# Feed-forward of a transformer layer: centred ternary weight, layer norm from the mean square, residual in one VectorE operation

## The chip, the cores and the metric

The kernel runs on one core of one Trainium2 chip. A core has a matrix engine (TensorE, "PE", with its weight loads listed as "PEld"), a vector engine (VectorE, "DVE"), an activation engine (ScalarE, "ACT"), a general engine (GpSimd, "POOL") and a queue that issues DMA transfers (SyncE, "SP"). Each engine works through its own list of instructions in order, and waits on semaphores where it needs another engine's result. The metric is the device time of one execution in microseconds.

## The reference, cut to what matters

The layer is an attention part followed by a feed-forward part. Only the feed-forward part, its layer norm and its residual are touched by the change:

```python
LN_EPS = 0.001; EPS = 1e-05; QB = 128.0
mu = jnp.mean(x, axis=-1, keepdims=True)
var = jnp.var(x, axis=-1, keepdims=True)
xn = (x - mu) * jax.lax.rsqrt(var + LN_EPS) * ln_gamma + ln_beta
beta = jnp.mean(jnp.abs(weight))
w_q = jnp.clip(ste_round(weight / (beta + EPS)), -1.0, 1.0)   # every weight is -1, 0 or 1
gamma = jnp.max(jnp.abs(xn))
xq = jnp.clip(xn * QB / gamma, -QB + EPS, QB - EPS)
y = jnp.einsum('bsd,du->bsu', xq, w_q)
return y * (gamma * beta / QB)

# around it, with x of shape (4, 4096, 512), float32
x = x + _layernorm(_L0_attn_ref(_layernorm(x), Wv, Wo, Wg, Wb))
x = x + _layernorm(_L0_ffn_ref(_layernorm(x), weight, ln_gamma, ln_beta))
```

`_layernorm` subtracts the mean over the last axis and divides by the root of the variance plus 1e-5.

## The kernel before, in words

The program has three stages, one after the other. `setup` loads the weights, splits the attention weights into two 16-bit parts, and makes the ternary weight `wq` (128 partitions x 4 x 512, 16 bit). `attention` makes the first residual sum and leaves it in DRAM (`x1_scratch`), with a scale and a shift for each row (`z_scale`) that stand for the layer norm ahead of the feed-forward part. `feed_forward` does the rest.

The 16,384 rows are 128 tiles of 128 rows x 512 columns. `feed_forward` takes them in 32 groups of G = 4 tiles. A group goes through these steps:

- load 1 MB of `x1` (SP, L1092), five steps ahead;
- `f_z` = x1 times scale plus shift, a tile at a time (DVE, L1230), three steps ahead;
- transpose `f_z` into the four banks `ps_z` (PE, L1273), two steps ahead, and from there scale by gamma and beta into `f_u` (ACT, L1151);
- one step ahead, the clip `f_uc` of the whole group (DVE, L1248, 128x2048), its 16-bit upper part (ACT, L1170) and the 16-bit remainder (DVE, L1259), both in `f_xq`;
- for each tile eight matmuls of 512 columns (4 blocks of the inner dimension, 2 parts) into one of the four banks `ps_f` (PE, L1285);
- the layer norm of `ps_f`: `bn_stats` and `bn_aggr` give mean and variance (DVE, L1209 and L1220); POOL makes the variance plus eps, the negated mean, the power -0.5 and the shift for two tiles at once (L1120, L1121, L1124, L1127); ACT applies scale and shift into `f_yn` (L1161); POOL adds the residual into `f_res` (L1133); SP stores `f_res` in four pieces (L1099).

The order of the work on each engine is written by hand in the functions `step`, and the semaphores named `f_...` count finished instructions. `step(base, j)` handles group j, and parts of groups j-1, j+1, j+2 and j+3. A matmul bank `ps_f[i]` is free again for the next group when ACT has written `f_yn` of tile i; PE starts a group when its remainder `f_lo` is there. The first 13 and the last 9 steps are written out and the 16 between run in a loop of 8.

Of the kernel before, what the change touches and what calls it, by code (L numbers as in the profile page):

```python
# [49 lines left out]
def setup(nc, io, k):  # L50

    with ExitStack() as ctx:
        def sb(name, shape, dt=F32):
# [20 lines left out]
        wo_mean = sb("wo_mean", [P, KB])  # L74
        above = sb("above", [P, KB, D])
# [9 lines left out]
        wo_summed, wo_meaned, wo_centred = sem("wo_summed"), sem("wo_meaned"), sem("wo_centred")  # L85

# [85 lines left out]
        def _(dve):  # L172
# [39 lines left out]

            dve.wait_ge(scaled, len(turns) + 1)
# [18 lines left out]
            dve.wait_ge(wq_s, 1)  # L232
# [789 lines left out]
def feed_forward(nc, io, k):  # L1022

    with ExitStack() as ctx:
# [3 lines left out]
        def sem(name):  # L1028
# [14 lines left out]
        sc = sb("f_sc", [P, 2, G, 2])  # L1043
# [4 lines left out]
        raw = sb("f_raw", [P, G, 6])  # L1048
        mv = sb("f_mv", [P, 2, G, 2])
        veps = sb("f_veps", [P, 2, 2])  # L1050
        neg = sb("f_neg", [P, 2, 2])
        ysc = sb("f_ysc", [P, 2, G, 2])
        yn = sb("f_yn", [P, G, D])
# [6 lines left out]
        names = """f_ends_g f_ends f_rowtop f_top f_inv f_scaled f_gb f_unit f_sc f_z f_zt f_u f_clip f_hi f_lo f_y  # L1060
            f_sums f_stats f_veps f_rstd f_ysc f_yn f_res""".split()
        s = {n: sem(n) for n in names}

        def run(eng, step):


            for j in range(-FLAG_LOAD, FBODY):
                step(None, j)
            with eng.Fori(1, NG // FBODY - 1) as base:
                for i in range(FBODY):  # L1070
                    step(base, i)
            for j in range(NG - FBODY, NG + 1):
                step(None, j)

        def on(base, step, lag):

            g = step + lag if base is None else base * FBODY + (step + lag)
            return g, (step + lag) % FBODY, not isinstance(g, int) or 0 <= g < NG
# [7 lines left out]
        @block.sync  # L1086
        def _(sp):
            def step(base, j):
                g, r, live = on(base, j, FLAG_LOAD)
                if live:  # L1090
                    wait(sp, s["f_res"], (g - (FBODY - 1)) * G)
                    sp.dma_start(x1[:, r, :, :], k["x1_dram"][bass.ds(g * G, G), :, :].rearrange("g p d -> p g d"))\  # L1092
                      .then_inc(loaded[r], 16)
                g, r, live = on(base, j, -1)
                if live:
                    sp.wait_ge(s["f_res"], g * G + G)
                    for b in range(B):
                        dst = io["out"][b, bass.ds(g * G * C, G * C), :].rearrange("(g t) d -> t g d", g=G)
                        sp.dma_start(dst, res[C * b:C * b + C, r % 2, :, :]).then_inc(stored[r % 2], 16)  # L1099
            run(sp, step)  # L1100
            for r in range(2):
                sp.wait_ge(stored[r], 16 * B * NG // 2)

        @block.gpsimd
        def _(pool):
# [4 lines left out]
            def half(base, j, lag, q):  # L1110

                g, r, live = on(base, j, lag)
                if not live:
                    return
                pair = slice(2 * q, 2 * q + 2)
                eps = y_eps[:, 0:1].to_broadcast([P, 2])

                pool.wait_ge(s["f_stats"], g * G + (2 * q + 2))
                wait(pool, s["f_yn"], (g - 1) * G)
                pool.tensor_tensor(veps[:, q, :], mv[:, r % 2, pair, 1], eps, ALU.add).then_inc(s["f_veps"], 1)  # L1120
                pool.tensor_tensor(neg[:, q, :], mv[:, r % 2, pair, 0], k["minus_one"][:, 0:1].to_broadcast([P, 2]),  # L1121
                                   ALU.mult).then_inc(s["f_veps"], 1)
                pool.wait_ge(s["f_veps"], g * 4 + (2 * q + 2))
                pool.tensor_tensor(ysc[:, r % 2, pair, 0], veps[:, q, :], k["neg_half"][:, 0:1].to_broadcast([P, 2]),  # L1124
                                   ALU.pow).then_inc(s["f_rstd"], 1)
                pool.wait_ge(s["f_rstd"], g * 2 + (q + 1))
                pool.tensor_tensor(ysc[:, r % 2, pair, 1], neg[:, q, :], ysc[:, r % 2, pair, 0], ALU.mult).then_inc(s["f_ysc"], 1)  # L1127

                for i in ((0,), (1, 2, 3))[q]:
                    pool.wait_ge(s["f_yn"], g * G + (i + 1))  # L1130
                    if i == 0 and (not isinstance(g, int) or g >= 2):
                        pool.wait_ge(stored[r % 2], (g - r % 2) * (8 * B))
                    pool.tensor_tensor(res[:, r % 2, i, :], yn[:, i, :], x1[:, r, i, :], ALU.add).then_inc(s["f_res"], 1)  # L1133

            def step(base, j):
                half(base, j, -1, 1)
                half(base, j, 0, 0)
            run(pool, step)

        @block.scalar  # L1140
        def _(act):
            act.wait_ge(s["f_gb"], 1)

            def inputs(base, j, blocks):

                g, r, live = on(base, j, FLAG_T)
# [7 lines left out]
            def outputs(base, j, lag, q):  # L1154

                g, r, live = on(base, j, lag)
                for i in (2 * q, 2 * q + 1) if live else ():
                    if i == 2 * q:
                        act.wait_ge(s["f_ysc"], g * 2 + (q + 1))
                    wait(act, s["f_res"], (g - 1) * G + (i + 1))  # L1160
                    nc.scalar.activation(yn[:, i, :], ps_f[i][:, :], ACT.Identity, scale=ysc[:, r % 2, i, 0:1],  # L1161
                                         bias=ysc[:, r % 2, i, 1:2]).then_inc(s["f_yn"], 1)

            def step(base, j):
                outputs(base, j, -1, 1)
                g, r, live = on(base, j, FLAG_CLIP)
# [4 lines left out]
                inputs(base, j, (0, 1))  # L1171
                outputs(base, j, 0, 0)
                inputs(base, j, (2, 3))
            run(act, step)

        @block.vector
        def _(dve):
# [24 lines left out]
            def sums(base, j, lag, i):  # L1202

                g, r, live = on(base, j, lag)
                if live:
                    dve.wait_ge(s["f_y"], g * G + (i + 1))
                    wait(dve, s["f_ysc"], g * 2 - 2)
                    wait(dve, s["f_stats"], (g - 1) * G + (i + 1))
                    dve.bn_stats(raw[:, i, :], ps_f[i][:, :]).then_inc(s["f_sums"], 1)  # L1209

            def summed(base, j, lag, i):

                g, r, live = on(base, j, lag)
                if live:
                    dve.wait_ge(s["f_sums"], g * G + (i + 1))

            def stats(base, j, lag, i):
                g, r, live = on(base, j, lag)
                if live:
                    dve.bn_aggr(mv[:, r % 2, i, :], raw[:, i, :]).then_inc(s["f_stats"], 1)  # L1220

            def norm(base, j, tiles):

                g, r, live = on(base, j, FLAG_Z)
# [8 lines left out]
            def step(base, j):
                sums(base, j, -1, 3)
                summed(base, j, -1, 3)
                g, r, live = on(base, j, FLAG_Z)
                if live:
                    wait(dve, s["f_z"], (g - 1) * G)
                    dve.tensor_copy(sc[:, r % 2, :, :].rearrange("p g c -> p (g c)"),
                                    k["z_scale"][:, bass.ds(g * (2 * G), 2 * G)]).then_inc(s["f_sc"], 1)  # L1240
                stats(base, j, -1, 2)
                stats(base, j, -1, 3)
                g, r, live = on(base, j, FLAG_CLIP)
# [5 lines left out]
                sums(base, j, 0, 0)  # L1249
                norm(base, j, (0, 1, 2))  # L1250
                sums(base, j, 0, 1)
                summed(base, j, 0, 1)
                norm(base, j, (3,))
                stats(base, j, 0, 0)
                stats(base, j, 0, 1)
# [4 lines left out]
                sums(base, j, 0, 2)  # L1260
            run(dve, step)

        @block.tensor
        def _(pe):
            def turn(base, j, kb):

                g, r, live = on(base, j, FLAG_T)
# [8 lines left out]
            def step(base, j):  # L1276
                g, r, live = on(base, j, 0)
                for i in range(G):
                    if live:
                        if i == 0:  # L1280
                            pe.wait_ge(s["f_lo"], g + 1)
                        wait(pe, s["f_yn"], (g - 1) * G + (i + 1))
# [5 lines left out]
                    turn(base, j, i)  # L1288
            run(pe, step)
# [43 lines left out]
```

## Time and profile before

| | |
|---|---|
| Time, median of 3 runs | 2510.26 us (2506.84 to 2511.02) |
| The profiled execution: its own time / its span | 2514.57 us / 2512.8 us |
| Busy share PE, DVE, ACT, POOL | 86%, 82%, 69%, 77% |
| Instructions | 146,586 |
| Mean granted TensorE clock | 0.945 of full |
| Feed-forward stage | from about 2055 us to the end of the span |

Times inside the span count from the span's start. "Busy" is the time in which an engine has an instruction in work; "idle before" is its time without one, put down to the last semaphore that released it. The page divides the span into 40 slices of 62.8 us; the feed-forward stage begins in the 33rd. Through most of attention PE's slices read nine tenths busy or more at the full clock. In the feed-forward stage they read seven or eight tenths, and the granted clock reads eight tenths.

### The profile page before, as it was taken

How to read it: one execution, taken by the hardware profiler on the slowest of the kernel's cores; microseconds unless marked ns; L12 is line 12 of the kernel's file. 1: busy time of each engine (PE TensorE's matmuls, PEld its weight loads, DVE VectorE, ACT ScalarE, POOL GpSimd, SP SyncE). 2: the span in 40 equal slices, each digit the busy share in tenths (PEclk: the TensorE clock that was granted, in tenths of full speed). 3: DMA queues.
4: the chain of work that ended last, by engine and by line, in shares of the span. 5: the costliest groups of instructions: out<-in, count | busy, mean ns of one | idle time of the engine just before them, and what ended most of it. 6: DMA issues, size and time to landing. Idle time of an engine off the chain costs nothing. (4 is left out here: it accounts for less than half of the span.)

```text
span 2512.8 us, 146586 instructions
## 1 busy us (share of the span) xinstructions
PE 2150.4 (86%) x61989; PEld 1350.3 (54%) x61989; DVE 2056.9 (82%) x5963; ACT 1739.4 (69%) x3500; POOL 1936.0 (77%) x3224
## 2 busy tenths in 40 slices
PE   1679999999999999998999999999998747787775
PEld 1356666566565666665666566666665523344442
DVE  4487998899888899988889898888998637777874
ACT  3767878777787778877887787778874335555554
POOL 1667888888788888888888888888886326777777
PEclk7789999999999999999999999999999768888888
DMA  2112222222222222222222222222222134556554
GB/s 81 50 43 59 80 75 79 77 74 75 71 80 76 75 73 80 80 72 75 80 77 73 74 80 78 74 76 80 77 63 69 46 128 124 153 152 165 151 135 100
DMA packets 132134, 215.47 MB, mean 86 GB/s; under 512 B 31352, under 2 KB 31360, under 8 KB 131488
## 3 DMA queue, kind: packets, MB, share of 16 engines
q1 hardware_dynamic: 131488, 206.20, 28.4%
q8 instruction: 486, 7.96, 1.4%
q14 instruction: 160, 1.31, 0.2%
HBM read 104.40 MB, written 67.11 MB: 68 GB/s over the span
## 5 line engine op out<-in xcount | busy, mean ns | idle before, releaser
L757 DVE TENSOR_TENSOR ps_elim<-ps_elim,sys 128x30 f32<-128x30 f32 (+14 forms) x1920 | 543.4, 326 | 0.8
L765 DVE TENSOR_TENSOR sys<-sys,ps_elim 128x30 f32<-128x30 f32 (+14 forms) x1920 | 534.8, 316 | 1.0
L882 PE MATMUL ps_v<-wv,xt 128*128 128x512 f16 x1536 | 433.6, 392 | 30.4 <-DMA kbd<-kt 17.2
L882 PE MATMUL ps_y<-wo,ot 128*128 128x512 f16 x1536 | 406.5, 388 | 9.5 <-DVE x L809 8.7
L1285 PE MATMUL ps_f<-wq,f_xq 128*128 128x512 f16 x1024 | 280.4, 424 | 103.0 <-ACT f_yn L1161 98.3
L909 PEld LDWEIGHTS ps_chain<-rhs,t_t 32*32 32x32 f32 x16384 | 262.9, 144 | 130.7 <-issue 129.2
L909 PE MATMUL ps_chain<-rhs,t_t 32*32 32x32 f32 x16384 | 294.9, 219 | 22.3 <-issue 16.3
L666 ACT ACTIVATE state<-ps_s 128x512 f32<-128x512 f32 x128 | 76.4, 597 | 268.8 <-PE ps_s L973 268.6
L903 PEld LDWEIGHTS ps_chain<-state,key_t 32*32 32x32 f32 x16384 | 175.2, 106 | 152.5 <-issue 151.6
L973 PEld LDWEIGHTS ps_s<-err,key_b 32*32 32x32 f32 x16384 | 172.7, 107 | 147.1 <-issue 146.7
L903 PE MATMUL ps_chain<-state,key_t 32*32 32x32 f32 x16384 | 211.3, 195 | 39.0 <-issue 38.4
L785 DVE TENSOR_TENSOR rhs<-val,ps_chain 128x512 f32<-128x512 f32 x128 | 88.0, 687 | 185.5 <-PE ps_chain L903 184.5
L973 PE MATMUL ps_s<-err,key_b 32*32 32x32 f32 x16384 | 206.6, 196 | 33.5 <-issue 33.5
L1285 PEld LDWEIGHTS ps_f<-wq,f_xq 128*128 128x128 f16 x1024 | 106.0, 106 | 227.2 <-issue 132.0
L1161 ACT ACTIVATE f_yn<-ps_f,f_ysc 128x512 f32<-128x512 f32 x128 | 92.5, 773 | 192.9 <-POOL f_ysc L1127 192.9
L882 PEld LDWEIGHTS ps_y<-wo,ot 128*128 128x128 f16 x1536 | 130.7, 98 | 118.9 <-issue 13.1
L882 PEld LDWEIGHTS ps_v<-wv,xt 128*128 128x128 f16 x1536 | 111.7, 99 | 151.4 <-issue 70.6
L1133 POOL TENSOR_TENSOR f_res<-f_yn,f_x 128x512 f32<-128x512 f32 x128 | 170.0, 1348 | 29.6 <-ACT f_yn L1161 29.6
L552 POOL TENSOR_TENSOR pred<-val,err 128x512 f32<-128x512 f32 x128 | 163.1, 1274 | 28.5 <-ACT err L645 28.5
L468 POOL TENSOR_TENSOR ln_mean<-ln_sum,mean_scales 128x2 f32<-128x2 f32 x128 | 24.7, 193 | 207.6 <-ACT unread_ln_sum L570 197.4
L538 POOL TENSOR_TENSOR m_t<-gram,b_mask 128x512 f32<-128x512 f32 x128 | 163.7, 1279 | 4.6 <-ACT gram L631 4.2
L930 PE MATMUL ps_gram<-kbd,kt 128*32 128x128 f32 x4096 | 153.0, 287 | 9.7 <-issue 9.7
(153 smaller groups left out, 5260.8 us busy)
## 6 DMA issues: line engine op xcount, KB each, us to landing
x_in<-in_L_attn_x SPq DMA_DIRECT2D x128, 256.0 KB
kbd<-kt SPq DMA_DIRECT2D x512, 64.0 KB
x_res<-in_L_attn_x SPq DMA_DIRECT2D x128, 256.0 KB
x_scratch<-x SPq DMA_DIRECT2D x128, 256.0 KB, 6.4
f_x<-x_scratch SPq DMA_DIRECT2D x32, 1024.0 KB, 7.6
out<-f_res SPq DMA_DIRECT2D x128, 256.0 KB, 3.9
gate<-gates SPq DMA_DIRECT2D x128, 7.9 KB
gate<-gates SPq DMA_DIRECT2D x128, 0.2 KB
```

The lines of the kernel that those rows point to most:

```text
L538: pool.tensor_tensor(m_t[:, :, l % 2, :], gram[:, :, :], b_mask[:, :, :], ALU.mult).then_inc(s["mt_done"], 1)
L552: pool.tensor_tensor(pred[:, :], val[:, l, :], err[:, l % 2, :], ALU.subtract).then_inc(s["pred_done"], 1)
L757: dve.tensor_tensor(tmp, factors(r, c, first, end)[:, c - first:C - 1 - first, c - first:c - first + 1].to_broadcast(shape), sys[:, r, c:c ...
L765: dve.tensor_tensor(dst, dst, tmp, ALU.add).then_inc(elim_done[r], 1)
L882: last = pe.matmul(out, lhs[:, a, kb, :], weights[:, w, kb, :], start=(i == 0), stop=(i == 3 * KB - 1))
L903: last = pe.matmul(ps_chain[q, e], key_t[q, l, h, :], state[q, l % 2, e], start=True, stop=True)
L909: last = pe.matmul(ps_chain[q, e], t_t[q, l // 2 % 2, :, l % 2, h], rhs[q, e], start=True, stop=True)
L930: last = pe.matmul(out, kt[:, m_l % 2, g, q], kbd[:, m_l % 2, :, g, q], start=True, stop=True)
L973: last = pe.matmul(ps_s[q, e], key_b[q, l, e], err[q, l % 2, e], start=(isinstance(n, int) and n == 0 and h == 0), stop=True, skip_group_c ...
L1133: pool.tensor_tensor(res[:, r % 2, i, :], yn[:, i, :], x1[:, r, i, :], ALU.add).then_inc(s["f_res"], 1)
L1161: nc.scalar.activation(yn[:, i, :], ps_f[i][:, :], ACT.Identity, scale=ysc[:, r % 2, i, 0:1], bias=ysc[:, r % 2, i, 1:2]).then_inc(s["f_yn ...
L1285: last = pe.matmul(ps_f[i][:, :], xq[:, r % 2, a, kb, P * i:P * i + P], k["wq"][:, kb, :], start=(m == 0), stop=(m == 2 * KB - 1))
```

## The change

In `setup`, the mean of each row of `wq` over its 512 columns is subtracted from it, still in 16 bits: one reduction, one small scaling and four additions on DVE. Since a row's sum is a whole number n, the centred value is a multiple of 1/512 below 2 and a 16-bit float holds it exactly. The matmul's result then has a mean of zero over its columns.

In `feed_forward`, ACT takes the mean square of each tile (`Square` with an accumulator, L1152 of the changed kernel), POOL adds eps and raises to -0.5 for one tile at a time (L1119, L1122), and one DVE operation does `f_res = ps_f * rstd + x1` (L1205). `bn_stats`, `bn_aggr`, the negated mean, the shift, the pass into `f_yn` and POOL's residual addition go. The copy of the row scales (`f_sc`) goes too: the loop over groups is written out in full, so they are read where they lie. A bank `ps_f[i]` is free for the next group when `f_res` of tile i is written.

```diff
+            dve.wait_ge(wq_s, 1)
+            dve.tensor_reduce(wq_sum[:, :], k["wq"][:, :, :], AX_X, ALU.add).then_inc(wq_summed, 1)
+            dve.wait_ge(wq_summed, 1)
+            dve.tensor_scalar(wq_mean[:, :], wq_sum[:, :], -1.0 / D, None, ALU.mult).then_inc(wq_meaned, 1)
+            dve.wait_ge(wq_meaned, 1)
+            for kb in range(KB):
+                dve.tensor_scalar(k["wq"][:, kb, :], k["wq"][:, kb, :], wq_mean[:, kb:kb + 1], None,
+                                  ALU.add).then_inc(wq_centred, 1)
...
-        def run(eng, step):
...
+        def run(step):
+            for j in range(-FLAG_LOAD, NG + 1):
+                step(j)
...
+            def rstd(j, lag, i):
+
+                g, r, live = on(j, lag)
+                if live:
+                    n, m = g * G + i, (g * G + i) % (2 * G)
+                    pool.wait_ge(s["f_var"], n + 1)
+                    wait(pool, s["f_rstd"], n - 2 * G + 1)
+                    pool.tensor_tensor(y_veps[:, m:m + 1], y_var[:, m:m + 1], y_eps[:, 0:1], ALU.add).then_inc(s["f_veps"], 1)
+                    pool.wait_ge(s["f_veps"], n + 1)
+                    wait(pool, s["f_res"], n - 2 * G + 1)
+                    pool.tensor_tensor(y_rstd[:, m:m + 1], y_veps[:, m:m + 1], k["neg_half"][:, 0:1],
+                                       ALU.pow).then_inc(s["f_rstd"], 1)
...
+            def squares(j, lag, i):
...
+                    act.wait_ge(s["f_y"], n + 1)
+                    wait(act, s["f_var"], n)
+                    wait(act, s["f_veps"], n - 2 * G + 1)
+                    nc.scalar.activation(unread[:, :], ps_f[i][:, :], ACT.Square, scale=D ** -0.5,
+                                         accum_out=y_var[:, m:m + 1]).then_inc(s["f_var"], 1)
+
+            def step(j):
+                inputs(j, FLAG_T - 1, (3,))
+                squares(j, -1, 3)
+                squares(j, 0, 0)
+                g, r, live = on(j, FLAG_CLIP)
                 if live:
                     act.wait_ge(s["f_clip"], g + 1)
                     wait(act, s["f_y"], (g - 1) * G)
                     nc.scalar.activation(xq[:, r % 2, 0, :, :], uc[:, :, :], ACT.Copy).then_inc(s["f_hi"], 1)
+                inputs(j, FLAG_T, (0,))
+                squares(j, 0, 1)
+                inputs(j, FLAG_T, (1,))
+                squares(j, 0, 2)
+                inputs(j, FLAG_T, (2,))
...
+            def output(j, lag, i):
...
+                    if i == 0 and g >= 2:
+                        dve.wait_ge(stored[r % 2], (g - r % 2) * (8 * B))
+                    dve.wait_ge(s["f_rstd"], n + 1)
+                    dve.scalar_tensor_tensor(out=res[:, r % 2, i, :], in0=ps_f[i][:, :], scalar=y_rstd[:, m:m + 1], in1=x1[:, r, i, :],
+                                             op0=ALU.mult, op1=ALU.add).then_inc(s["f_res"], 1)
...
-                        wait(pe, s["f_yn"], (g - 1) * G + (i + 1))
+                        wait(pe, s["f_res"], (g - 1) * G + (i + 1))
```

On DVE one step of the feed-forward stage stood like this before, from one remainder (`f_xq`) to the next clip and on to the transforms `f_z`:

```order
L1259 TENSOR_TENSOR f_xq<-f_uc,f_xq 128x2048
L1209 BN_STATS f_raw<-ps_f 128x6 x2
L1239 COPY f_sc<-z_scale 128x8
L1220 BN_AGGR f_mv<-f_raw 128x2 x2
L1248 TENSOR_SCALAR f_uc<-f_u 128x2048
L1209 BN_STATS f_raw<-ps_f 128x6
L1230 TENSOR_SCALAR f_z<-f_x,f_sc 128x512 x3
L1209 BN_STATS f_raw<-ps_f 128x6
L1230 TENSOR_SCALAR f_z<-f_x,f_sc 128x512
L1220 BN_AGGR f_mv<-f_raw 128x2 x2
```

It now stands like this (DVE, the same stretch of a step; the three `f_res` ahead of the clip are tiles 1 and 2 of group j and tile 3, the one behind the two `f_z` is tile 0 of the next group):

```order
L1232 TENSOR_TENSOR f_xq<-f_uc,f_xq 128x2048
L1205 SCALAR_TENSOR_TENSOR f_res<-ps_f,f_y_rstd,f_x 128x512
L1216 TENSOR_SCALAR f_z<-f_x,z_scale 128x512 x2
L1205 SCALAR_TENSOR_TENSOR f_res<-ps_f,f_y_rstd,f_x 128x512 x2
L1226 TENSOR_SCALAR f_uc<-f_u 128x2048
L1216 TENSOR_SCALAR f_z<-f_x,z_scale 128x512 x2
L1205 SCALAR_TENSOR_TENSOR f_res<-ps_f,f_y_rstd,f_x 128x512
```

Four `f_res` took the place of four `bn_stats`, four `bn_aggr` and the copy, and two of the four `f_z` moved from behind the clip to behind the remainder. On ACT, a step of before, from the upper part `f_xq` on:

```order
L1170 ACTIVATE f_xq<-f_uc 128x2048
L1151 ACTIVATE f_u<-ps_z,f_gb 128x512
L1161 ACTIVATE f_yn<-ps_f,f_ysc 128x512 x2
L1151 ACTIVATE f_u<-ps_z,f_gb 128x512
```

ACT now alternates between the two banks' kinds, and the fourth `f_u` stands ahead of the squares of tile 3 and of the next group's tile 0:

```order
L1163 ACTIVATE f_xq<-f_uc 128x2048
L1141 ACTIVATE f_u<-ps_z,f_gb 128x512
L1152 ACTIVATE f_unread,f_y_var<-ps_f 128x512
L1141 ACTIVATE f_u<-ps_z,f_gb 128x512
L1152 ACTIVATE f_unread,f_y_var<-ps_f 128x512
L1141 ACTIVATE f_u<-ps_z,f_gb 128x512 x2
L1152 ACTIVATE f_unread,f_y_var<-ps_f 128x512 x2
```

Every square stands behind at least one `f_u`, and the squares of tiles 1 and 2 stand behind the upper part.

## Rows read from the trace of the kernel before

**Rows 1.** The chain of waits, feed-forward stage: start us, us, engine and line.
```profile
2209.70 0.70 POOL f_ysc L1124
...
2220.89 2.15 POOL f_veps L1120
2223.27 0.70 POOL f_ysc L1124
...
2439.47 0.70 POOL f_ysc L1124
...
2466.45 0.70 POOL f_ysc L1124
...
2477.93 0.70 POOL f_ysc L1124
```

**Rows 2.** Timeline of one step: start us, us, engine, line, what [idle before].
```profile
2211.71 3.57 PE L1285 MATMUL ps_f<-wq,f_xq 128*128 128x512 f16 x8 [3.15 <-ACT f_yn L1161]
...
2213.28 1.58 POOL L1124 TENSOR_TENSOR f_ysc<-f_veps,neg_half 128x2 f32<-128x2 f32 x1
2213.60 1.23 DVE L1248 TENSOR_SCALAR f_uc<-f_u 128x2048 f32<-128x2048 f32 x1 [2.42 <-ACT f_u L1151]
...
2216.09 3.38 DVE L1230 TENSOR_SCALAR f_z<-f_x,f_sc 128x512 f32<-128x512 f32 x3
2216.59 1.91 ACT L1170 ACTIVATE f_xq<-f_uc 128x2048 f16<-128x2048 f32 x1
...
2217.71 1.89 PE L1285 MATMUL ps_f<-wq,f_xq 128*128 128x512 f16 x8
...
2219.87 1.89 PE L1285 MATMUL ps_f<-wq,f_xq 128*128 128x512 f16 x8
...
2220.73 2.26 DVE L1259 TENSOR_TENSOR f_xq<-f_uc,f_xq 128x2048 f16<-128x2048 f32 x1
```

**Rows 3.** Groups by line, 2050 us to the end: busy, mean ns | idle before.
```profile
L1133 POOL TENSOR_TENSOR f_res<-f_yn,f_x 128x512 f32<-128x512 f32 x128 | 170.0, 1348 | 29.6 <-ACT f_yn L1161 29.6
L1230 DVE TENSOR_SCALAR f_z<-f_x,f_sc 128x512 f32<-128x512 f32 x128 | 130.2, 1059 | 1.3
...
L1151 ACT ACTIVATE f_u<-ps_z,f_gb 128x512 f32<-128x512 f32 x128 | 92.8, 778 | 17.7 <-PE ps_z L1273 17.5
...
L1209 DVE BATCH_NORM_STATS2 f_raw<-ps_f 128x6 f32<-128x512 f32 x128 | 85.5, 688 | 16.4 <-PE ps_f L1285 15.3 <-POOL f_ysc L1127 0.8
...
L1220 DVE BATCH_NORM_AGGREGATE f_mv<-f_raw 128x2 f32<-128x6 f32 x128 | 15.4, 162 | 0.2
```

**Rows 4.** Timeline, start of the feed-forward stage, while POOL does nothing.
```profile
2066.48 1.92 DVE L1230 TENSOR_SCALAR f_z<-f_x,f_sc 128x512 f32<-128x512 f32 x4
```

**Rows 5.** Timeline, last tiles of attention, lines 578 to 809.
```profile
2044.85 0.60 ACT L578 ACTIVATE unread_y_var<-ps_y 128x512 f32<-128x512 f32 x1 [0.70 <-PE ps_y L882]
2045.34 0.19 ACT L578 ACTIVATION_READ_ACCUMULATOR unread_y_var<-ps_y 128x1 f32 x1
...
2045.62 0.19 POOL L496 TENSOR_TENSOR y_sc<-y_var,attn_eps 128x1 f32<-128x1 f32 x1 [3.29 <-ACT unread_y_var L578]
2045.88 0.55 POOL L498 TENSOR_TENSOR y_sc<-y_sc,neg_half 128x1 f32<-128x1 f32 x1
...
2046.66 0.75 DVE L809 SCALAR_TENSOR_TENSOR x<-ps_y,y_sc,x_res 128x512 f32<-128x512 f32 x1 [3.47 <-POOL y_sc L498]
2046.79 0.55 POOL L516 TENSOR_TENSOR z_scale<-z_veps,neg_half 128x1 f32<-128x1 f32 x1
```

**Rows 6.** Busy time by stretch: PE, PEld, DVE, ACT, POOL, clock, DMA share, GB/s.
```profile
2055.00:2078.00 23.00, 5.32 (x32) 5.08 (x32) 14.16 (x28) 6.95 (x9) 0.38 (x1) 0.64 0.89 319
...
2090.00:2200.00 110.00, 82.57 (x389) 43.14 (x390) 85.13 (x120) 60.95 (x75) 86.45 (x100) 0.88 0.56 148
```

**Rows 7.** Timeline of the setup stage, DVE.
```profile
25.76 2.29 DVE L214 TENSOR_REDUCE wo_sum<-wt_o 128x4 f32<-128x2048 f32 x1 [2.57 <-ACT wt_g L165]
...
28.28 1.67 DVE L219 TENSOR_SCALAR wt_o<-wt_o,wo_mean 128x512 f32<-128x512 f32 x4
```

More of the change, by code:

```diff
@@ L231, in _ @@
             dve.wait_ge(lo_s, 3)
-            dve.wait_ge(wq_s, 1)
+            dve.wait_ge(wq_centred, KB)
 LAG_LOAD = 13
@@ L1047, in feed_forward @@
         xq = sb("f_xq", [P, 2, 2, KB, G * P], F16)
[L1048 to L1053, printed above, removed]
+        unread = sb("f_unread", [P, D])
+        y_var = sb("f_y_var", [P, 2 * G])
+        y_veps = sb("f_y_veps", [P, 2 * G])
+        y_rstd = sb("f_y_rstd", [P, 2 * G])
         res = sb("f_res", [P, 2, G, D])
@@ L1059, in feed_forward, with on @@
         stored = [sem(f"f_stored{i}") for i in range(2)]
-        names = """f_ends_g f_ends f_rowtop f_top f_inv f_scaled f_gb f_unit f_sc f_z f_zt f_u f_clip f_hi f_lo f_y
-            f_sums f_stats f_veps f_rstd f_ysc f_yn f_res""".split()
+        names = """f_ends_g f_ends f_rowtop f_top f_inv f_scaled f_gb f_unit f_z f_zt f_u f_clip f_hi f_lo f_y
+            f_var f_veps f_rstd f_res""".split()
         s = {n: sem(n) for n in names}
-        def run(eng, step):
[L1067 to L1078, printed above, removed]
+        def run(step):
+            for j in range(-FLAG_LOAD, NG + 1):
+                step(j)
+        def on(step, lag):
+            g = step + lag
+            return g, g % FBODY, 0 <= g < NG
         def wait(eng, semaphore, count):
-            if not isinstance(count, int) or count > 0:
+            if count > 0:
                 eng.wait_ge(semaphore, count)
@@ L1108, in _ @@
             pool.wait_ge(s["f_unit"], 3)
[L1110 to L1133, printed above, removed]
@@ L1140, in _, with step @@
+            def step(j):
+                for i in range(G):
+                    rstd(j, 0, i)
+            run(step)
         @block.scalar
@@ L1152, in inputs, with step @@
                                          bias=gb[:, KB + kb:KB + kb + 1]).then_inc(s["f_u"], 1)
[L1154 to L1166, printed above, removed]
+            def squares(j, lag, i):
+                g, r, live = on(j, lag)
+                if live:
+                    n, m = g * G + i, (g * G + i) % (2 * G)
+                    act.wait_ge(s["f_y"], n + 1)
[3 more added lines that the diff above has]
+                                         accum_out=y_var[:, m:m + 1]).then_inc(s["f_var"], 1)
+            def step(j):
+                inputs(j, FLAG_T - 1, (3,))
+                squares(j, -1, 3)
+                squares(j, 0, 0)
+                g, r, live = on(j, FLAG_CLIP)
                 if live:
@@ L1200, in _, with norm @@
                                      op0=ALU.mult, op1=ALU.mult).then_inc(s["f_unit"], 1)
-            def sums(base, j, lag, i):
-                g, r, live = on(base, j, lag)
+            def output(j, lag, i):
+                g, r, live = on(j, lag)
                 if live:
[L1206 to L1224, printed above, removed]
+                    n, m = g * G + i, (g * G + i) % (2 * G)
+                    if i == 0 and g >= 2:
[3 more added lines that the diff above has]
+                                             op0=ALU.mult, op1=ALU.add).then_inc(s["f_res"], 1)
+            def norm(j, tiles):
+                g, r, live = on(j, FLAG_Z)
                 for i in tiles if live else ():
@@ L1228, in norm, with step @@
                         wait(dve, s["f_zt"], (g - 1) * KB)
-                        dve.wait_ge(s["f_sc"], g + 1)
-                    dve.tensor_scalar(z[:, r % 2, i, :], x1[:, r, i, :], sc[:, r % 2, i, 0:1], sc[:, r % 2, i, 1:2],
+                    sc = k["z_scale"][:, (g * G + i) * 2:(g * G + i) * 2 + 2]
+                    dve.tensor_scalar(z[:, r % 2, i, :], x1[:, r, i, :], sc[:, 0:1], sc[:, 1:2],
                                       ALU.mult, ALU.add).then_inc(s["f_z"], 1)
[L1233 to L1243, printed above, removed]
+            def step(j):
+                output(j, -1, 3)
+                g, r, live = on(j, FLAG_CLIP)
                 if live:
@@ L1248, in step @@
                     dve.tensor_scalar(uc[:, :, :], u[:, :, :], QB - Q_EPS, -(QB - Q_EPS), ALU.min, ALU.max).then_inc(s["f_clip"], 1)
[L1249 to L1255, printed above, removed]
+                norm(j, (0, 1))
+                output(j, 0, 0)
                 if live:
@@ L1259, in step, with turn @@
                     dve.tensor_tensor(xq[:, r % 2, 1, :, :], uc[:, :, :], xq[:, r % 2, 0, :, :], ALU.subtract).then_inc(s["f_lo"], 1)
-                sums(base, j, 0, 2)
-            run(dve, step)
+                output(j, 0, 1)
+                norm(j, (2, 3))
+                output(j, 0, 2)
+            run(step)
         @block.tensor
         def _(pe):
-            def turn(base, j, kb):
-                g, r, live = on(base, j, FLAG_T)
+            def turn(j, kb):
+                g, r, live = on(j, FLAG_T)
                 if live:
```

36 lines of the change are left out of this document (15 added, 21 removed).

## The prediction, made before the changed kernel ran

> **What bounds the kernel now.** I read the page first: the three stages follow each other, attention is not touched by the change, and setup and feed-forward are. So I read the feed-forward stage on its own. The chain of waits through it is regular: POOL's power -0.5 (`f_ysc`, L1124) comes back at 2209.70 and at 2439.47 with 16 others between them, so one group of four tiles takes 229.77 / 17 = 13.52 us [rows 1]. After the last `f_z` the period is 2477.93 - 2466.45 = 11.48 us [rows 1].
>
> In that period no engine is busy all the time: in 110 us PE works 82.57, DVE 85.13, ACT 60.95, POOL 86.45, all near 78% or less [rows 6]. It is a loop of waits, not a full engine. Three things in it matter. (a) POOL's small addition `f_veps` is asked for just after DVE started the remainder `f_xq`, and ends when that ends: DVE works from 2220.73 to 2222.99, POOL's addition lasts 2.15 us to 2223.04 [rows 1, 2], where an addition of this kind otherwise takes 0.19 [rows 5]. (b) three of DVE's `f_z` take 3.38 us side by side with POOL's residual addition, on average 1.06 us each beside POOL's 1.35 [rows 2, 3], and 0.48 each while POOL does nothing [rows 4]. (c) PE waits 3.15 us for `f_yn` to free a bank, and its next eight matmuls take 3.57 us in place of 1.89 [rows 2]; the clock over this stretch is 0.88 of 2.4 GHz, a mean of its two levels [rows 6].
>
> **The change part by part, feed-forward.** Removed per group on DVE: four `bn_stats` of 0.69, four `bn_aggr` of 0.16 and the small copy; on ACT four `f_yn`; on POOL four residual additions of 1.35 and eight small operations. Added on DVE: four `f_res`, each one pass over a matmul bank with a column scale and an operand from SBUF. Attention has the same operation with an accumulator output (L809), 0.75 us [rows 5]; the other bound is `bn_stats`, a pass over the same bank without a second operand, 0.69 [rows 3]. I take 0.75. Added on ACT: four squares with accumulator, the same as L578, 0.60 plus a read of 0.19 that overlaps, next instruction 0.59 after the start [rows 5]. Added on POOL for each tile: an addition of 0.19 and a power of 0.55 [rows 5]. From the start of a square to the start of the DVE operation that uses it, attention takes 2046.66 - 2044.85 = 1.81 us [rows 5]; I use that.
>
> With POOL's long additions gone, `f_z` falls to 0.48. Its bounds are 0.48 [rows 4] and 1.06 [rows 3]; the short POOL work left (0.74 us per tile) is nearer to the first. DVE's own work per group is then 4 x 0.75 + 4 x 0.48 + 1.23 + 2.26 = 8.4 us, ACT's 4 x 0.72 + 4 x 0.59 + 1.9 = 7.1 us (0.72 is 92.8 us over 128 `f_u`), and PE's at full clock 4 x (2219.87 - 2217.71 = 2.16) = 8.64 us [rows 2, 3, 5].
>
> The Trainium skill (SBUF — State Buffer, Who interferes with whom) says that a DVE instruction with at most one SBUF input and outside the two-port modes does not contend with GpSimd. The trace agrees: POOL's power takes its usual 0.55 us beside L809 [rows 5]. By that rule `f_res` neither delays POOL nor is delayed; without it each `f_res` could cost up to 0.55 more, 2.2 us per group.
>
> Now the order on DVE, walked from the start of the clip at 0. Clip 1.23 [rows 2]; hand-over 0.05; upper part on ACT 1.91 [rows 2]; hand-over 0.05; so the remainder starts at 3.24 and ends at 5.50. Meanwhile DVE does two `f_z` and `f_res` of tile 0, 1.7 us, which fits in the 2.0 that it would wait. Queued behind the remainder is `f_res` of tile 1. Its square stands on ACT behind the upper part (3.19) and an `f_u`, is done at about 4.6, and POOL's addition then falls into the remainder, where by (a) it is held until 5.50. From there: power starts 0.28 later (2223.27 against 2222.99), 0.55 long, 0.23 to DVE as from L498 to L809 [rows 1, 2, 5]: `f_res` of tile 1 starts at 6.56. DVE is idle for 1.06 us there; this is the new wait. Then 0.75, two `f_z` 0.96, `f_res` of tile 2 0.75: 9.02. Tile 3's square starts on ACT at 3.19 + 4 x 0.72 + 2 x 0.59 = 7.25, so its `f_res` may start at 9.06. It ends at 9.81, and the next clip starts. One period is 9.8 us.
>
> PE starts the next group at 5.5, needs 8.64 and is idle for 1.2 us. Its banks are free in time: `f_res` of tile 1 ends at 7.3, and PE wants that bank at 5.5 + 2.16 = 7.7. Between 9.8 and 13.5 lie 3.7 us per group.
>
> DMA: 2.1 MB per group, in and out, is 214 GB/s at 9.8 us. The stage runs at 148 GB/s with the DMA engines 56% busy, and its start reaches 319 [rows 6]. A store has over a period until its buffer is wanted. I count nothing, and bound it under the rivals.
>
> The loop written out in full costs fetches of code that the trace can show: before, its straight part ran 13.49 us a group (2439.47 to 2466.45, two groups) and the part with the loop 13.52 [rows 1]. I count zero.
>
> **Setup.** Added on DVE: a reduction over 2048 columns, 2.29, a small scaling, 0.2, and four additions, at most 1.67 as the same four in 32 bits [rows 7]; together 4.2 us. DVE was idle for 2.57 us just behind `wq`, waiting for ACT [rows 7]. So 1.6 us are left on the path, about 1.0 if the 16-bit additions take half.
>
> **The sum**, against the profiled execution (2514.57 us, span 2512.8): 28.5 full periods (2078 to 2466.45) x 3.7 = 106 us; the last two steps without `f_z`, from 11.48 to about 9.4 each, 4; the last group, whose matmuls no longer wait for banks, 2; its ending: before, `bn_stats`, `bn_aggr`, small work of 1.3, `f_yn` and three additions on POOL, together some 6.5, now 1.81 + 0.75 = 2.6, so 4. Minus 1.6 for setup: 114 us faster. 2514.6 - 114 = 2400.6. The profiled execution is 4.3 us above the median of the runs, 2510.3; from there it is 2396. I forecast 2397.
>
> **The rivals.**
> 1. PE sets the period. Per group it was busy 82.57 x 13.52 / 110 = 10.15 us at clock 0.88 [rows 6]. If the short waits in the new order keep the clock there, a group takes 10.3 us instead of 9.8: 28.5 x 0.5 = 14 us less gained, 2411. For it: every group still begins behind an idle 1.2 us. Against it: after the idle time in rows 2 the slow matmuls followed a wait of 3.15 us, and PE would be some 88% busy. The Trainium skill (TensorE: Matmul & The Clock Gate, A second HAM failure mode: psum-queue depth-cycling) warns of just this, short idle times between groups of matmuls that take turns in banks making the clock swing between its levels; by that rule it would be this 2411.
> 2. POOL's small operations are caught by DVE's two-operand and fast operations more often than once a group. The power of 0.55 becomes 1.58 when a clip starts in it (2213.28, clip at 2213.60) [rows 2]. If one more `f_res` in each group waits for that, the period is 10.8: 2397 + 28.5 = 2425.
> 3. The new idle time is not there, because ACT or POOL get tile 1 through ahead of the remainder: 9.8 - 1.06 = 8.7, where PE's 8.64 plus a wait makes it about 9.0: 2397 - 23 = 2374.
> 4. DMA becomes the bound. If it could not go above the stage's own 148 GB/s by more than a tenth, 2.1 MB take 12.9 us: 28.5 x 3.1 = 88, 2485. Against it: 319 GB/s at the start.
> 5. Slower than before: the granted clock falls to 1.2 GHz for the stage. Eight matmuls then take 3.57 [rows 2] and the four transposes behind them twice 0.27, 4 x 4.1 = 16.4 us a group. It decides from the point where PE's group passes 13.5 us, a mean clock of about 0.65; the price is 28.5 x 2.9 = 83, giving 2593. Against it: PE idles less than before.
> 6. The change does not do what it says: if centring made the weight 32 bit, the matmuls would cost several times as much. But `wq` stays declared 16 bit and PE's instructions are the same.
>
> **How the numbers follow.** Forecast (period 9.5 to 10.1, 2387 to 2406) 0.48; rival 1 0.18; rival 2 0.15; rival 3 0.11; rival 4 0.04; rival 5 0.02; anything else 0.02. Holding 8 in 10: the unknown sizes, `f_res` at 0.69 (minus 0.24 a group, 7 us) and `f_z` between 0.48 and 1.06 on the two that no wait hides (up to 1.2 a group, 33 us), fall into it: 2377 to 2430. Beyond 0.2%, which is about what a measurement of this kernel can tell from no change, faster has 0.96, same 0.01, slower 0.03.
>
> **What would show it.** `f_z` near 0.5 us each and no POOL operation above 2.3 us; POOL's addition for tile 1 held to the end of the remainder, with DVE idle about 1 us behind it; the mean period of the remainders 9.8; PE idle 1 us per group at a clock near 1.0; DVE's `f_res` 0.70 to 0.75; in setup no idle time of DVE before the reduction of `wo`, and attention starting 1 to 2 us later. It is wrong if DVE waits for tile 0 or 3, if `f_z` stays near 1 us, if the stores hold `f_res`, or if the clock stays at 0.88.

## The result, and the profile after

The changed kernel takes 2372.3 us (median of 4 runs, 2363.5 to 2378.8) against 2510.6 us before in the same job (4 runs, 2506.8 to 2513.7). The ratio is 0.945, 95% interval 0.942 to 0.949. The forecast was 2397 us, in a range of 2377 to 2430: the direction was right, the time lies below the range. The profiled execution took 2363.5 us.

The changed kernel's page, span and slices (tenths busy, granted clock, DMA share, GB/s):

```profile
span 2361.7 us, 145902 instructions
...
PE   1679999999999999999999999999999987399997
...
PEclk7789999999999999999999999999999997799999
DMA  2111222222222222222222222222222221478885
GB/s 81 50 49 55 80 74 78 76 76 77 76 76 76 77 76 79 77 77 81 74 78 77 77 73 78 77 75 82 77 76 77 60 60 49 152 198 232 228 230 130
```

The feed-forward stage begins in the 35th of these slices. From the 36th to the 39th PE is now nine tenths busy or more and the granted clock reads nine tenths or more, and from the 37th to the 39th DMA moves some 230 GB/s. The busy time over one stretch (as in [rows 6]) and the groups by line (as in [rows 3]; the last is from the page):

```profile
2200.00:2300.00 100.00, 96.03 (x523) 53.61 (x523) 87.47 (x108) 75.48 (x141) 41.08 (x86) 1.00 0.87 229
```
```profile
L1205 DVE SCALAR_TENSOR_TENSOR f_res<-ps_f,f_y_rstd,f_x 128x512 f32<-128x512 f32 x128 | 95.7, 748 | 31.5 <-POOL f_y_rstd L1122 30.0
...
L1152 ACT ACTIVATE f_unread<-ps_f 128x512 f32<-128x512 f32 x128 | 76.9, 601 | 11.4 <-PE ps_f L1260 8.6 <-issue 0.4
...
L1216 DVE TENSOR_SCALAR f_z<-f_x,z_scale 128x512 f32<-128x512 f32 x128 | 63.5, 540 | 0.0
...
L1119 POOL TENSOR_TENSOR f_y_veps<-f_y_var,y_eps 128x1 f32<-128x1 f32 x128 | 53.6, 418 | 175.5 <-ACT f_unread L1152 174.6
```

`f_res` takes 0.75 us, the square 0.60 and `f_z` 0.54 (two in 0.99), where `f_z` was 1.06. Now one group, in the timeline of the changed kernel, from one clip to the next:

```profile
2201.73 1.22 DVE L1226 TENSOR_SCALAR f_uc<-f_u 128x2048 f32<-128x2048 f32 x1
...
2202.98 1.91 ACT L1163 ACTIVATE f_xq<-f_uc 128x2048 f16<-128x2048 f32 x1 [2.15 <-DVE f_uc L1226]
...
2204.80 0.76 ACT L1141 ACTIVATE f_u<-ps_z,f_gb 128x512 f32<-128x512 f32 x1
2204.92 2.29 DVE L1232 TENSOR_TENSOR f_xq<-f_uc,f_xq 128x2048 f16<-128x2048 f32 x1 [0.40 <-ACT f_xq L1163]
...
2205.46 0.58 ACT L1152 ACTIVATE f_unread<-ps_f 128x512 f32<-128x512 f32 x1
...
2206.03 0.77 ACT L1141 ACTIVATE f_u<-ps_z,f_gb 128x512 f32<-128x512 f32 x1
2206.21 1.05 POOL L1119 TENSOR_TENSOR f_y_veps<-f_y_var,y_eps 128x1 f32<-128x1 f32 x1 [4.40 <-ACT f_unread L1152]
2206.69 0.60 ACT L1152 ACTIVATE f_unread<-ps_f 128x512 f32<-128x512 f32 x1
...
2207.26 1.46 ACT L1141 ACTIVATE f_u<-ps_z,f_gb 128x512 f32<-128x512 f32 x2
2207.34 0.55 POOL L1122 TENSOR_TENSOR f_y_rstd<-f_y_veps,neg_half 128x1 f32<-128x1 f32 x1
...
2207.93 0.75 DVE L1205 SCALAR_TENSOR_TENSOR f_res<-ps_f,f_y_rstd,f_x 128x512 f32<-128x512 f32 x1 [0.71 <-POOL f_y_rstd L1122]
...
2208.58 0.62 ACT L1152 ACTIVATE f_unread<-ps_f 128x512 f32<-128x512 f32 x1
2208.59 0.99 DVE L1216 TENSOR_SCALAR f_z<-f_x,z_scale 128x512 f32<-128x512 f32 x2
...
2209.51 1.54 DVE L1205 SCALAR_TENSOR_TENSOR f_res<-ps_f,f_y_rstd,f_x 128x512 f32<-128x512 f32 x2
2209.64 0.66 PE L1248 MATMUL ps_z<-ident,f_z 128*128 128x128 f32 x4 [0.36 <-DVE f_z L1216]
2209.71 0.55 POOL L1122 TENSOR_TENSOR f_y_rstd<-f_y_veps,neg_half 128x1 f32<-128x1 f32 x1
...
2210.96 1.22 DVE L1226 TENSOR_SCALAR f_uc<-f_u 128x2048 f32<-128x2048 f32 x1
```

The period is 2210.96 - 2201.73 = 9.23 us, and it stays 9.23 (clips at 2090.93 and 2183.26, ten periods apart, give 9.233). The order of events is the predicted one: POOL's addition for tile 1 is held until the remainder ends (2207.21; the addition ends at 2207.26), and DVE is idle behind it, for 0.71 us.

Two links close the loop here. DVE's `f_res` of tile 2 ends near 2210.17; POOL's power for tile 3 ends at 2210.26. They differ by 0.1 us, and `f_res` of tile 3 starts at 2210.30, just behind the later one. The first comes by DVE's own queue, the second by ACT: clip, upper part, then `f_u` and squares in turn up to the square of tile 3 at 2208.58. Here ACT's chain ended last. The next clip stands behind `f_res` of tile 3 and so behind both.

### The profile page after: what moved, and what is told of

The parts are those of the page before. It is cut to its first block and busy times, and to the rows that moved or that the text cites. A ratio compares the mean times of both kernels' runs of the same rounds, so it can differ in the third digit from the quotient of the medians.

```text
span 2361.7 us, 145902 instructions
## 1 busy us (share of the span) xinstructions
PE 2096.4 (89%) x61989; PEld 1329.8 (56%) x61989; DVE 1985.9 (84%) x5809; ACT 1726.4 (73%) x3628; POOL 1725.6 (73%) x3096
## 5 line engine op out<-in xcount | busy, mean ns | idle before, releaser
L894 PE MATMUL ps_v<-wv,xt 128*128 128x512 f16 x1536 | 428.5, 389 | 24.6 <-DMA kbd<-kt 12.6
L1260 PE MATMUL ps_f<-wq,f_xq 128*128 128x512 f16 x1024 | 242.6, 381 | 6.8 <-DVE f_xq L1232 6.8
L894 PEld LDWEIGHTS ps_y<-wo,ot 128*128 128x128 f16 x1536 | 130.1, 98 | 119.2 <-issue 12.3
L1119 POOL TENSOR_TENSOR f_y_veps<-f_y_var,y_eps 128x1 f32<-128x1 f32 x128 | 53.6, 418 | 175.5 <-ACT f_unread L1152 174.6
L1260 PEld LDWEIGHTS ps_f<-wq,f_xq 128*128 128x128 f16 x1024 | 100.3, 98 | 101.9 <-DVE f_xq L1232 7.5
L517 POOL TENSOR_TENSOR x_part<-x_hat,x_part 128x512 f16<-128x512 f32 x128 | 148.5, 1160 | 5.6 <-ACT x_part L617 3.1
```

Source lines behind the costliest of these rows:

```text
L517: pool.tensor_tensor(x_part[:, l % 2, 1, :], x_hat[:, l % 4, :], x_part[:, l % 2, 0, :], ALU.subtract).then_inc(s["xlo_done"], 1)
L894: last = pe.matmul(out, lhs[:, a, kb, :], weights[:, w, kb, :], start=(i == 0), stop=(i == 3 * KB - 1))
L1119: pool.tensor_tensor(y_veps[:, m:m + 1], y_var[:, m:m + 1], y_eps[:, 0:1], ALU.add).then_inc(s["f_veps"], 1)
L1260: last = pe.matmul(ps_f[i][:, :], xq[:, r % 2, a, kb, P * i:P * i + P], k["wq"][:, kb, :], start=(m == 0), stop=(m == 2 * KB - 1))
```

## The experiments

Periods are from clip to clip over at least four groups (eight in most). The "stage" is the time from the reduction `f_top` near the end of attention to the span's end: 454.5 us before, 322.2 after.

**Centring alone**, in the kernel before:

```diff
+            dve.tensor_reduce(wq_sum[:, :], k["wq"][:, :, :], AX_X, ALU.add)...
...
-            dve.wait_ge(wq_s, 1)
+            dve.wait_ge(wq_centred, KB)
```


> The kernel before with the weight's centring in setup and nothing else. Theory A (the whole gain is in the feed-forward stage, setup costs what is left after DVE's idle 2.57 us): attention starts 0.9 us later, the rest is as before, time 2511 to 2512, period of a group 13.5 us. Theory B (something in the setup or the centred weight also shortens attention, which was about 15 us shorter in the changed kernel's profile): attention 10 us or more shorter, time near 2500.

Measured: ratio to before 1.001 (0.998 to 1.003), period 13.52, stage 456.7. Theory A holds. **The changed kernel without centring** (its last layer norm then leaves out the mean):

```diff
-            dve.tensor_reduce(wq_sum[:, :], k["wq"][:, :, :], AX_X, ALU.add)...
...
+            dve.wait_ge(wq_s, 1)
```


> The changed kernel without the centring of the weight (the subtraction of the mean in the last layer norm is left out). Theory A: setup is 0.9 us shorter, everything else as in the changed kernel, period 9.23 us, time 2371. Theory B (the centring is what makes attention shorter): attention 10 to 15 us longer, 2383 or more.

Measured: 2370.3 us, 0.944 (0.940 to 0.947), period 9.23, stage 324.2. Theory A holds, and centring costs next to nothing; in the changed kernel's setup its rows are:

```profile
23.05 2.29 DVE L217 TENSOR_REDUCE wq_sum<-wq 128x4 f32<-128x2048 f16 x1
...
25.58 1.14 DVE L222 TENSOR_SCALAR wq<-wq,wq_mean 128x512 f16<-128x512 f16 x4
...
26.63 2.28 DVE L226 TENSOR_REDUCE wo_sum<-wt_o 128x4 f32<-128x2048 f32 x1
```

The reduction of `wo` starts at 26.63 in place of 25.76 [rows 7]: 0.9 us. In the run without centring it starts at 25.48, 1.15 us earlier.

**The loop written out**, all else as before:

```diff
-            with eng.Fori(1, NG // FBODY - 1) as base:
...
+            for j in range(-FLAG_LOAD, NG + 1):
+                step(None, j)
```


> The kernel before with the feed-forward groups written out in full instead of a loop of 8, all its operations kept. Theory A (the loop cost nothing, as its straight part ran at the same 13.5 us a group): time within 3 us of the kernel before. Theory B (registers and branches of the loop were part of the 13.5 us, or straight code costs fetches): 5 us or more away, faster or slower.

Measured: 2508.3 us, 0.999 (0.997 to 1.001), period 13.50, stage 453.8. Theory A holds.

**Statistics back on DVE**, single output operation kept:

```diff
-                    nc.scalar.activation(unread[:, :], ps_f[i][:, :], ACT.Square, ...)
+                    dve.bn_stats(raw[:, i, :], ps_f[i][:, :]).then_inc(s["f_sums"], 1)
+                    dve.bn_aggr(mv[:, m, :], raw[:, i, :]).then_inc(s["f_var"], 1)
```


> The changed kernel with bn_stats and bn_aggr on DVE in place of the squares on ACT; single f_res operation, centred weight and POOL's two small operations kept. Theory A (the loop is now set by DVE's own work and ACT's chain at nearly the same length): DVE gets 4 x (0.61 + 0.16) = 3.1 us more per group, its work becomes 11.0 us, period 11.2 to 12, time 2372 + 28.5 x 2.3 = 2437 (2428 to 2450). So of the 4.3 us per group gained, about half is the move of the statistics to ACT. Theory B (DVE's idle time of 1.2 us per group and ACT's relief take most of it): period under 10.3, time under 2402.

Measured: 2476.1 us, 0.987 (0.983 to 0.991), period 12.46, stage 420.8. That is 3.2 us more per group, where theory A had at most 2.8, and the time lies 26 us above its range: A's direction holds, its size doesn't, and B is out. DVE's work is near the 11.0 us expected (86% of 12.46 is 10.8), but two waits for POOL stand in it (here for tile 3 and for tile 0):

```profile
2206.75 0.75 DVE L1192 SCALAR_TENSOR_TENSOR f_res<-ps_f,f_y_rstd,f_x 128x512 f32<-128x512 f32 x1 [0.93 <-POOL f_y_rstd L1124]
...
2210.98 0.75 DVE L1192 SCALAR_TENSOR_TENSOR f_res<-ps_f,f_y_rstd,f_x 128x512 f32<-128x512 f32 x1 [0.78 <-POOL f_y_rstd L1124]
```

**Output in two parts again**, squares on ACT kept:

```diff
-                    dve.scalar_tensor_tensor(out=res..., in0=ps_f..., scalar=y_rstd..., in1=x1...)
+                    nc.scalar.activation(yn[:, i, :], ps_f[i][:, :], ACT.Copy, scale=y_rstd[:, m:m + 1])
+                    pool.tensor_tensor(res[:, r % 2, i, :], yn[:, i, :], x1[:, r, i, :], ALU.add)
```


> The changed kernel with the output in two parts as before: ACT scales the bank into f_yn (which also frees the bank), POOL adds the residual; the squares on ACT and the centred weight stay. Theory A (the single DVE operation earns by taking 2.9 us from ACT and 5.2 us from POOL, and f_z back to 0.5 us): ACT's work becomes 10.1 us a group, f_z 1.06 to 1.35, period 11.5 to 13, time 2437 to 2480. Theory B (only the removal of bn_stats and bn_aggr from DVE matters, 3.1 to 3.4 us): period near 9.5 to 10.3, under 2402.

Measured: 2451.3 us, 0.975 (0.971 to 0.979), period 11.46, stage 393.0. The time is in A's range and the period just below it, but not for its reasons: `f_z` stays at 0.54. The clip and the remainder pay, here in this kernel's timeline:

```profile
2203.19 2.16 DVE L1238 TENSOR_SCALAR f_uc<-f_u 128x2048 f32<-128x2048 f32 x1 [2.13 <-ACT f_u L1153]
...
2208.86 2.76 DVE L1243 TENSOR_TENSOR f_xq<-f_uc,f_xq 128x2048 f16<-128x2048 f32 x1 [2.59 <-ACT f_xq L1185]
```

The clip takes 2.16 us (1.22 in the changed kernel) and the remainder 2.76 (2.29), each while a POOL addition runs beside it (2202.99 to 2204.26 and 2208.19 to 2209.46), and DVE waits 2.13 and 2.59 us for the longer ACT.

**One more POOL addition per tile**, read by nobody, in the changed kernel:

```diff
+                    pool.tensor_tensor(extra[:, :], k["gamma_bc"][:, :], k["beta_bc"][:, :], ALU.add)
```


> The changed kernel with one more POOL addition of 128x512 per tile, on constants and read by nobody, behind each tile's power: POOL's load of before without its place in the loop. Theory A (POOL's long additions made f_z slow, and that was a large part of the old period): f_z goes back to 1.0 to 1.35 us, DVE's work rises by about 2.3 us a group, period 11.5 to 13, time 2437 or more. Theory B (the contention costs only little time, it was the waits for POOL's results that mattered): f_z slow but period under 10.3, time under 2402.

Measured: 2458.3 us, 0.977 (0.972 to 0.981), period 11.67. The period is A's, its cause is not: `f_z` takes 0.60, not 1.0 to 1.35. Most of the cost is the queue: the power of the next tile stands behind the long addition. Groups by line of this kernel:

```profile
L1208 DVE SCALAR_TENSOR_TENSOR f_res<-ps_f,f_y_rstd,f_x 128x512 f32<-128x512 f32 x128 | 96.1, 751 | 89.2 <-POOL f_y_rstd L1123 85.3
...
L1219 DVE TENSOR_SCALAR f_z<-f_x,z_scale 128x512 f32<-128x512 f32 x128 | 71.5, 601 | 0.0
```

DVE's idle time ahead of `f_res` is 89 us where it was 31.5, some 1.8 us of the 2.4 that a group got longer. The rest is in the operations that run beside one of POOL's additions, here the clip (1.22 before) and the second pair of `f_z` (0.99 before), in the timeline:

```profile
2204.35 1.62 DVE L1229 TENSOR_SCALAR f_uc<-f_u 128x2048 f32<-128x2048 f32 x1
...
2211.61 1.28 DVE L1219 TENSOR_SCALAR f_z<-f_x,z_scale 128x512 f32<-128x512 f32 x2
```

This run also answers whether the granted clock earned the gain: over 2200 to 2300 us it is 1.00 here as in the changed kernel, and a group still takes 11.67 us. A full clock alone doesn't bring the 9.23.

**Order on DVE, three variants** of the changed kernel, with the changed kernel again, all in one job:

```diff
             def step(j):
-                output(j, -1, 3)
                 ... clip ...
+                output(j, -1, 3)
```


> The changed kernel with one exchange on DVE: the clip of the next group stands ahead of f_res of tile 3 instead of behind it. Theory A (DVE and ACT chains tie at 9.23 us, and both run through f_res of tile 3 into the clip): the loop without that link has DVE work of about 8.5 us, so PE's 4 x 2.16 = 8.65 us sets the period; 28.5 x 0.58 = 16.5 us faster than the changed kernel, about 2355. Theory B (PE's wait for f_z or the hold behind the remainder sets it): period stays 9.1 to 9.2, time 2369 to 2372.


```diff
-                output(j, 0, 1)
                 norm(j, (2, 3))
+                output(j, 0, 1)
                 output(j, 0, 2)
```


> The changed kernel with the two f_z that stand behind f_res of tile 1 put ahead of it, into DVE's wait of 0.71 us behind the remainder. Theory A (ACT's chain clip, upper part, three f_u and squares in turn, square of tile 3, POOL, f_res of tile 3, clip is as long as DVE's): only DVE's side gets shorter, the period falls by 0.13 us to 9.10, 4 us in all, 2368. Theory B (the hold behind the remainder is on the path, as the prediction had it): the period falls by up to 0.58 us to PE's 8.65, 2355.

Both exchanges together:

> Both exchanges at once. Theory A: PE sets the period in either case, 8.65 us, 2355, no different from the clip put first alone. Theory B: it is the only one of the three that reaches 8.65, the single exchanges stay near 9.1 to 9.2.

The changed kernel again:

> The changed kernel itself once more. Theory A (attention's length varies from execution to execution by some 10 us either way, whatever the kernel; the first profile of the changed kernel had a short one): feed-forward from its first DVE operation to the end again 322 to 324 us, attention's end anywhere between 2039 and 2058 us, median 2370 to 2378. Theory B (the changed kernel has a shorter attention for a reason): attention ends near 2040 us again.

| kernel | median us | ratio to before (95%) | period | stage |
|---|---|---|---|---|
| changed, again | 2382.2 | 0.9475 (0.945 to 0.950) | 9.24 | 324.4 |
| `f_z` behind the remainder | 2379.1 | 0.9446 (0.943 to 0.947) | 9.17 | 320.9 |
| clip first | 2364.5 | 0.9406 (0.938 to 0.944) | 8.75 | 306.8 |
| both | 2358.9 | 0.9391 (0.936 to 0.942) | 8.67 | 303.9 |

By the periods, filling the wait of 0.71 us wins 0.06 us (the times alone can't tell it from the changed kernel, their intervals overlap): DVE then waits for POOL ahead of tile 3 instead, in the timeline of that kernel:

```profile
2208.67 0.75 DVE L1205 SCALAR_TENSOR_TENSOR f_res<-ps_f,f_y_rstd,f_x 128x512 f32<-128x512 f32 x1 [0.58 <-POOL f_y_rstd L1122]
```

Taking the clip out from behind tile 3 wins 0.48 us, and both win 0.57, down to PE's 8.66 (four times its 2.16). Theory A holds for the link that counts, but the three kernels show one thing that it left out: clip first alone stopped 0.09 short of PE's pace. There once a group a transpose still has to wait for the `f_z` behind the wait for POOL, in the timeline of clip first:

```profile
2202.84 0.42 PEld L1248 LDWEIGHTS ps_z<-ident,f_z 128*128 128x128 f32 x4 [0.37 <-DVE f_z L1216]
```

With both exchanges PE is never idle (busy time in the stretch, kernel with both). Clip first alone reads 100.00 too, so the busy share can't tell the two apart; the period can:

```profile
2200.00:2300.00 100.00, 100.00 (x556) 57.77 (x555) 92.94 (x116) 82.19 (x153) 66.55 (x92) 1.00 0.91 242
```

This version is faster than both kernels; its interval doesn't meet the changed kernel's of the same job. The changed kernel itself took 2382.2 us, above the 2370 to 2378 that theory A expected, but the kernel before was slower in this job too, 2518.7 against 2510.6. On attention, theory A holds: the changed kernel's attention ended (`f_top`) at 2039.5 us in its first profile and at 2050.6 here:

```profile
L1181 DVE TENSOR_REDUCE f_top<-f_ends x1: 1220/1220/1220, 2050.6 to 2050.6; 128x1 f32<-128x1024 f32 x1
```

Over all 14 profiles, of 13 kernels, it lies between 2039.5 and 2065.3 us, with no clear pattern in what was changed.

**The hand-over from POOL to DVE.** The prediction took 0.23 us from attention [rows 5]; `f_res` starts 0.04 us after the power. Two trials:

```diff
+                    for name in ("f_var", "f_veps", "f_y", "f_zt"):
+                        dve.wait_ge(s[name], 1)
```


> The changed kernel with four more waits ahead of each f_res, all on counts long reached. Theory A (the hand-over from POOL to DVE was 0.23 us in attention and is 0.04 us here because L809 waits for five semaphores and f_res for one): the hand-over becomes 0.2 us again, once or twice on the path of a group, period 9.4 to 9.6, time 5 to 11 us longer, 2377 to 2383. Theory B (waits already met cost nothing): period 9.23, time unchanged.


```diff
-                                             op0=ALU.mult, op1=ALU.add)
+                                             op0=ALU.mult, op1=ALU.add, accum_out=sums[:, n:n + 1])
```


> The changed kernel with an accumulator output on each f_res (the sums are read by nobody), which makes it the form of attention's L809. Theory A (the 0.23 us from the end of POOL's power to the start of L809 belongs to the form with accumulator, against 0.04 us for the form without): f_res of tile 1 starts 0.2 us after its power ends, the period rises by about 0.2 to 0.4 us a group to 9.4 to 9.6. Theory B (it belongs to something else in attention): 0.04 us again, the period rises by no more than the accumulator reads, 0 to 0.08 us per f_res.

Measured: with four more waits 2380.4 us (0.9475, 0.943 to 0.952), period 9.23; with the accumulator one run of 2383.1, period 9.26. In the second, the timeline:

```profile
2208.03 0.55 POOL L1123 TENSOR_TENSOR f_y_rstd<-f_y_veps,neg_half 128x1 f32<-128x1 f32 x1
...
2208.61 0.75 DVE L1206 SCALAR_TENSOR_TENSOR f_res<-ps_f,f_y_rstd,f_x 128x512 f32<-128x512 f32 x1 [0.71 <-POOL f_y_rstd L1123]
```

Again 0.03 us. Theory B both times: neither the waits nor the accumulator by itself makes attention's 0.23; what does stays open.

## Why the prediction was wrong

**The step that failed is a term of the sum: "One period is 9.8 us".** The loop and the order of its events came as predicted; the term measured 9.23 us. 28.5 x 0.57 = 16 us. The walk had two chains that end within 0.04 us of each other at `f_res` of tile 3, ACT's at 9.06 and DVE's at 9.02, and it priced both too high, so that mending one of them would have left the sum at 9.8. The later one, ACT's, set the number. Counted from the clip:

| ACT's chain | walk | trace |
|---|---|---|
| first `f_u` behind the upper part | 3.19 | 2204.80, 3.07 |
| square of tile 3, behind four `f_u` and two squares | 7.25 | 2208.58, 6.85 |
| `f_res` of tile 3 | 9.06 | 2210.30, 8.57 |
| next clip | 9.81 | 2210.96, 9.23 |

The same kind of joint is wrong on both engines:

- It added whole durations where one instruction follows another. The records overlap. An `f_u` of 0.76 to 0.77 us has the next instruction 0.66 behind its start (2204.80, 2205.46), where the walk took 0.72, and the upper part of 1.91 has it 1.82 behind (2202.98, 2204.80). `f_res` lasts 0.75 but the next starts 0.66 behind it (2207.93, 2208.59). On DVE three such joints make 0.22 us.
- From the end of the remainder to the power it took 0.28 us, a figure from before in which another POOL operation stood between. It is 0.13 (2207.21 to 2207.34). The rows had what was missing: attention's addition ends at 2045.81 and its power starts at 2045.88 [rows 5].
- From the end of the power to `f_res` it took 0.23; it is 0.04. Together with the joint before it this makes DVE's idle time 0.71 instead of 1.06: 0.35 us. On ACT's chain the same hand-over is part of the 1.81 us from square to `f_res`, which measured 1.72.

The overlap could be seen before: L809 starts at 2046.66 and lasts 0.75 [rows 5], and the next operation starts 0.68 behind it; a remainder of 2.26 us has the next operation 2.18 behind its start. Both from the timeline of the kernel before:

```profile
2047.34 0.69 DVE L817 TENSOR_TENSOR z_ends<-ps_zn,z_ends 128x512 f32<-128x512 f32 x1
...
2207.16 2.26 DVE L1259 TENSOR_TENSOR f_xq<-f_uc,f_xq 128x2048 f16<-128x2048 f32 x1
...
2209.34 1.29 DVE L1209 BATCH_NORM_STATS2 f_raw<-ps_f 128x6 f32<-128x512 f32 x2
```

**The range was too narrow below**: rival 3 (2374) was put down to a wait that would vanish, and took the whole 1.06 us off, though ACT's chain at 9.06 would have kept the period. The wait is there, and a period below 9.8 came from the joints, to which no bound was given. A period of 9.2 is 17 us below the forecast; taken off the range's lower end, it would have begun near 2360.

**Attention was taken as fixed.** It varies by 10 us either way between executions, more than the 0.2% (5 us) that the chances took as what can be told from no change. The stage shrank by 454.5 - 322.2 = 132.3 us, and by 130.1 in the second profile of the changed kernel, against 116 forecast; the 16 us of the period close that gap. The first job's medians differ by 138 us, the second's by 136.5; after 0.9 for setup, some 5 to 9 us are left. Attention's variation is large enough to cover them, but that is argued, not shown: the run without centring and the one with four more waits, each against the kernel before of its own job, leave some 10 and 4 us of the same sign, which chance alone explains poorly. What they are stays open.

**What was right**: no `bn_stats` and no long POOL addition, `f_z` at 0.5, the hold of POOL's addition by the remainder, DMA far beyond 148 GB/s (rival 4), and a full clock: it is 1.00 over the stretch, with idle times of 0.36 us between groups of matmuls, so rival 1 did not come true. What the Trainium skill (TensorE: Matmul & The Clock Gate, A second HAM failure mode: psum-queue depth-cycling) warns of did not happen in this trace. Setup cost 0.9 us, the "about 1.0" of the prediction's text and not the 1.6 of its sum.

**What was right by luck**: "this is the new wait" was on DVE's side only. ACT's chain ran as long as DVE's, which the walk had but did not weigh: filling the wait is worth 0.06 us a group. The prediction also had PE start free of `f_z`; in fact its first transposes wait 0.36 us for the `f_z` just made, which costs next to nothing at 9.23, where PE has 0.58 to spare, and 0.09 us a group once the clip goes first.

**Where the 4.29 us per group came from.** With squares on ACT alone (two-part output) a group takes 11.46, with the single output alone (statistics on DVE) 12.46, with both 9.23, with neither 13.52. Apart they give 2.1 and 1.1 us, together 4.3, so each takes away something that the other leaves standing. With squares alone POOL is busy 92% of a stretch (2200 to 2300 us) and DVE waits for ACT; with the single output alone DVE is busy 86% and waits for POOL. Those two kernels have orders of their own, so the split is rough.

## What to carry to other kernels

Where a loop of waits sets the pace, look for the instruction at which two chains meet, here `f_res` of tile 3 ahead of the clip, and take that link out. Filling the largest idle gap helped little as long as the other chain was as long. If two chains of a walk end within a hundredth or two of the period of each other, price both. In a walk along an in-order queue, take the start-to-start distance of such instructions from the trace, not the duration: over a dozen joints it is the difference between a forecast and a miss.

## What the runs showed that was not expected

- How many additions POOL has doesn't say what they cost DVE; which DVE operation runs at the same time does. `f_z` was 1.06 us in the kernel before, beside POOL's additions, and 0.60 and 0.54 with as many of them in two other orders, where it runs beside them for a short while or not at all; there the power behind the addition, or the clip (1.62 and 2.16 for 1.22), paid.
- In the stage's own traffic DMA reached 242 GB/s with its engines 91% busy in the fastest version. It may be the next limit, close behind PE, but no run tests it, and the start of the stage before moved 319 GB/s at a share of 0.89 [rows 6].
- An instruction that waits for five semaphores, four of them long reached, started no later than one that waits for one (9.23 us a group against 9.23 and 9.24).
